# 64x64 products in all four corners of the PE array, and the decay of both recurrent states moved to ScalarE

## The reference

```python
def step(carry, inp):
    S, R = carry
    q_t, k_t, v_t, a_t, aR_t, b_t, g_t = inp
    kn = k_t / jnp.maximum(jnp.linalg.norm(k_t, axis=-1, keepdims=True), 1e-12)
    pred = jnp.einsum('bhji,bhj->bhi', S, kn)
    r = jnp.clip(v_t - pred, -CLIP, CLIP)
    S = a_t[..., None] * S
    kp = jnp.einsum('bhd,bhde->bhe', kn, S)
    S = S + b_t[..., None, None] * kn[..., None] * (v_t - kp)[..., None, :]
    o = jnp.einsum('bhji,bhj->bhi', S, q_t)
    R = aR_t[..., None] * R
    kpR = jnp.einsum('bhd,bhde->bhe', kn, R)
    R = R + g_t[..., None, None] * kn[..., None] * (r - kpR)[..., None, :]
    o = o + jnp.einsum('bhji,bhj->bhi', R, q_t)
    return ((S, R), o)
```

## Time and profile before

| | us |
|---|---|
| median of 3 runs | 3591.83 (3588.75 to 3591.98) |
| time of the profiled execution | 3588.82 |
| its span, first to last instruction | 3587.0 |
| of it the 32 chunks of the scan, about | 60 to 2690 |
| TensorE's mean granted clock, share of full speed | 0.911 |
| PE / DVE / ACT / POOL busy over the span | 88% / 76% / 48% / 34% |

### The profile page before, as it was taken

One profiled execution on the slowest core, in us unless ns is written; L12 is line 12 of the kernel. 1 busy time (PEld: TensorE's weight loads), 2 busy tenths in 40 slices (PEclk: granted clock), 3 DMA queues, 4 the chain that ended last, 5 costly groups with the idle time before them and its releaser, 6 DMA issues. The chain is left out here.

```text
span 3587.0 us, 134780 instructions
## 1 busy us (share of the span) xinstructions
PE 3170.7 (88%) x56922; PEld 2864.8 (80%) x56922; DVE 2724.0 (76%) x6995; ACT 1715.9 (48%) x4108; POOL 1212.5 (34%) x1001
## 2 busy tenths in 40 slices
PE   4999999999999999999999999999973998888880
PEld 4988888888888888888888898898862776667660
DVE  3888888899888888889888888888872444444445
ACT  2444554444444445544445444554421655555550
POOL 3112322222222223222222222322211666666664
PEclk8999899999999998999999999899985999999995
DMA  3211111111111111111111111111118777777766
GB/s 113 81 53 34 40 34 36 41 35 36 41 37 33 34 40 34 37 35 41 34 37 43 34 34 34 40 34 37 40 46 317 118 116 113 113 114 113 115 109 203
DMA packets 193472, 240.09 MB, mean 67 GB/s; under 512 B 26737, under 2 KB 171250, under 8 KB 192114
## 3 DMA queue, kind: packets, MB, share of 16 engines
q1 hardware_dynamic: 132896, 151.22, 13.7%
q0 software_dynamic: 58368, 75.80, 13.2%
q10 hardware_dynamic: 1618, 4.46, 0.3%
HBM read 96.17 MB, written 135.20 MB: 65 GB/s over the span
## 5 line engine op out<-in xcount | busy, mean ns | idle before, releaser
L383 POOL DMA_INDIRECT table<-xrow,place_i x256 | 264.1, 1032 | 800.1 <-DVE BR L846 191.7
L1080 POOL COPY inv_r<-N 32x512 f32<-32x512 f32 x128 | 136.5, 1067 | 798.7 <-DVE N L822 794.7
L1450 PE MATMUL bank<-w,route 128*128 x2560 | 371.3, 288 | 34.9 <-issue 10.8
L1450 PEld LDWEIGHTS bank<-w,route 128*128 128x128 f32 x2560 | 312.4, 192 | 104.2 <-issue 101.3
L449 DVE TENSOR_TENSOR tri<-tri,step 128x58 f32<-128x58 f32 (+13 forms) x896 | 305.4, 341 | 30.8
L448 DVE TENSOR_TENSOR step<-tri 128x58 f32<-128x58 f32 (+13 forms) x896 | 301.6, 337 | 26.4
L1465 PE MATMUL bank<-w,seen 128*128 x640 | 214.4, 417 | 51.2 <-DVE sh_sig L1538 9.7
L1526 DVE COPY to_row<-shared 128x1 int32<-128x1 int32 x228 | 35.1, 154 | 269.8 <-DMA acc<-sh_sig,to_row 39.5
L578 PE MATMUL bank<-xnT,wa 128*128 128x128 f32 x992 | 155.0, 330 | 67.5 <-ACT xnT L962 67.5
L578 PEld LDWEIGHTS bank<-xnT,wa 128*128 128x128 f32 x992 | 149.1, 242 | 71.6 <-ACT xnT L962 71.6
L637 PE MATMUL bank<-pq,c 64*64 64x128 f32 x2048 | 168.5, 339 | 0.0
(11 more groups left out here) (306 smaller groups left out, 9086.8 us busy)
## 6 DMA issues: line engine op xcount, KB each, us to landing
table<-blank SPq DMA_DIRECT2D x320, 129.0 KB
shared<-table SPq DMA_DIRECT2D x228, 129.0 KB
w<-in_wpack_dram SPq DMA_DIRECT2D x16, 1540.0 KB
xrow<-table SPq DMA_DIRECT2D x92, 129.0 KB
sum<-acc SPq DMA_DIRECT2D x16, 512.0 KB
acc<-blank SPq DMA_DIRECT2D x33, 128.0 KB, 3.1
x_rows<-y SPq DMA_DIRECT2D x64, 64.0 KB
x_res<-in_x_dram SPq DMA_DIRECT2D x64, 64.0 KB
```

Of the source, the lines that this page charges most:

```text
L383: nc.gpsimd.indirect_dma_start(out=table, out_offset=bass.IndirectOffsetOnAxis(ap=t.place8_i[:, k:k + 1], axis=0), in_=row[:, :], in_offse ...
L1080: ins = nc.gpsimd.tensor_copy(t.inv[1][r, :, Q * (q % 2):Q * (q % 2) + Q], t.N[r, 16:32, :])
L1450: mm = nc.tensor.matmul(ps[:, begin:begin + n], t.xT_slot[i % 3][:, P * kt:P * kt + P], weights(i, 257 * kt + begin, n), start=(kt == 0), ...
```

## The change

Products with 64x64 tiles are put in all four corners. `four` replaces `accumulate` and, for KS, KR, U, PR, W, A, O and RO, also `units`: it takes two banks at once and alternates between them. Every second unit (s = 1) is crossed: half j writes the partitions of the other half. for KS, KR, U, PR, W and A even units go to bank 0 and odd ones, crossed, to bank 1 (`crossed`). V, KRt, B ahead of U, BR, L and the inverses then hold their odd units with the halves exchanged, and the crossed groups U and W bring them back. For O and RO units 4a and 4a+1 go to bank 0 and 4a+2 and 4a+3, crossed, to bank 1. SU, RU, RQ, KT and PQ stay as they were. Copies and DVE operations that empty a bank address every second unit (`even_odd`) or every second pair of units (`by_pair`). V, the gates, `wo` and the bias are laid out to match. PR now waits for both U banks, RO for both W banks, and W for both halves of BR.

The two decays (DVE, lines 866 and 878) become `decay_state` on ACT: 16 activations of 128x64 each, with the decay of the unit as per-partition scale. The one of S stands behind the copies of O and ahead of the diagonal blocks, that of R behind the diagonal blocks and ahead of the copies of V.

```diff
--- before.py
+++ after.py
...
@@ -543,16 +552,33 @@
...
 
-            def accumulate(ps, h, pairs, first=False, last=False):
-
-                for i, u in enumerate(range(8 * h, 8 * h + 8)):
+            def four(banks, unit, pairs, first=True, last=True, whole=False):
+
+                for i in range(8):
                     for m, (lhsT, rhs) in enumerate(pairs):
-                        for j in range(2):
-                            r = slice(C * j, C * j + C)
-                            mm = nc.tensor.matmul(ps[r, C * i:C * i + C], lhsT(r, u), rhs(r, u),
-                                                  start=(first and i == 0 and m == 0),
-                                                  stop=(last and i == 7 and m == len(pairs) - 1))
-                return mm
+                        begin, end = m == 0, m == len(pairs) - 1
+                        if whole:
+                            begin, end = first and i == 0 and begin, last and i == 7 and end
+                        for s in range(2):
+                            u = unit(i, s)
+                            for j in range(2):
+                                r, to = slice(C * j, C * j + C), slice(C * (j ^ s), C * (j ^ s) + C)
+                                mm = nc.tensor.matmul(banks[s][to, C * i:C * i + C], lhsT(r, u), rhs(r, u),
+                                                      start=begin, stop=end)
+                            if s == 0:
+                                ins = mm
+                return ins, mm
+
+            def odd_unit(i, s):
+                return 2 * i + s
+
+            def pair_unit(i, s):
+                return 4 * (i // 2) + 2 * s + i % 2
+
+            def crossed(n, name, pairs):
+                banks = [begin(n, f"{name}0"), begin(n, f"{name}1")]
+                for ins in four(banks, odd_unit, pairs):
+                    ins.then_inc(t.sem["mm_done"], 1)
 
...
@@ -608,15 +634,13 @@
...
                 need(pe, t, "states_ready", 2 * n - 1)
-                for h in range(2):
-                    units(n, f"KS{h}", h, [(of(t.kplus[0]), of(t.S))])
+                crossed(n, "KS", [(of(t.kplus[0]), of(t.S))])
                 if front:
...
                 need(pe, t, "states_ready", 2 * n)
-                for h in range(2):
-                    units(n, f"KR{h}", h, [(of(t.kplus[1]), of(t.R))])
+                crossed(n, "KR", [(of(t.kplus[1]), of(t.R))])
                 if front:
...
@@ -678,12 +702,10 @@
...
                 pe.wait_ge(t.sem["inv_s_ready"], n + 1)
-                for h in range(2):
-                    units(n, f"U{h}", h, [(of(t.inv[0]), of(t.B))])
-                for h in range(2):
-                    wait_emptied(pe, t, o, n, f"U{h}")
-                    units(n, f"PR{h}", h, [(lambda r, u: t.pq[r, 0, u, :], of(t.S)),
-                                           (lambda r, u: t.pqT[r, u, 0, :], of(t.U))])
+                crossed(n, "U", [(of(t.inv[0]), of(t.B))])
+                wait_emptied(pe, t, o, n, "U1")
+                crossed(n, "PR", [(lambda r, u: t.pq[r, 0, u, :], of(t.S)),
+                                  (lambda r, u: t.pqT[r, u, 0, :], of(t.U))])
                 for h in range(2):
...
@@ -691,22 +713,20 @@
...
                         norm_matmul(nc, t, ps, i).then_inc(t.sem["front_mm"], 1)
-                for h in range(2):
-                    ins = accumulate(begin(n, f"O{h}"), h, [(of(t.S), lambda r, u: t.pq[r, 1, u, :]),
-                                                            (of(t.R), of(t.rqplus)),
-                                                            (of(t.U), lambda r, u: t.pqT[r, u, 1, :])], first=True)
-                ins.then_inc(t.sem["O_begun"], 1)
+                O = [begin(n, "O0"), begin(n, "O1")]
+                ins = four(O, pair_unit, [(of(t.S), lambda r, u: t.pq[r, 1, u, :]), (of(t.R), of(t.rqplus)),
+                                          (of(t.U), lambda r, u: t.pqT[r, u, 1, :])], last=False, whole=True)
+                ins[1].then_inc(t.sem["O_begun"], 1)
                 ps = begin(n, "SD")
...
                 pe.wait_ge(t.sem["inv_r_ready"], n + 1)
-                for h in range(2):
-                    pe.wait_ge(t.sem["BR_ready"], 2 * n + h + 1)
-                    units(n, f"W{h}", h, [(of(t.inv[1]), of(t.BR))])
-                for h in range(2):
-                    wait_emptied(pe, t, o, n, f"W{h}")
-                    accumulate(o.bank(t, n, f"O{h}"), h, [(of(t.B), of(t.rqT))], last=True).then_inc(t.sem["O_done"], 1)
+                pe.wait_ge(t.sem["BR_ready"], 2 * n + 2)
+                crossed(n, "W", [(of(t.inv[1]), of(t.BR))])
+                wait_emptied(pe, t, o, n, "W1")
+                for ins in four(O, pair_unit, [(of(t.B), of(t.rqT))], first=False, whole=True):
+                    ins.then_inc(t.sem["O_done"], 1)
                 for h in range(2):
...
@@ -789,7 +809,7 @@
...
                     ps = mm(n, f"KS{h}")
-                    nc.vector.tensor_tensor(t.B[:, half[h], :], t.V[:, half[h], :], blk(ps[:, :]),
+                    nc.vector.tensor_tensor(even_odd(t.B, h), even_odd(t.V, h), blk(ps[:, :]),
                                             ALU.subtract).then_inc(t.sem["dve_emptied"], 1)
...
@@ -835,15 +855,15 @@
...
                 for h in range(2):
-                    r, rest = t.BR[:, half[h], :], t.KRt[:, half[h], :]
+                    r, rest = even_odd(t.BR, h), even_odd(t.KRt, h)
                     ps = mm(n, f"PR{h}")
-                    nc.vector.tensor_tensor(r, t.V[:, half[h], :], blk(ps[:, :]),
+                    nc.vector.tensor_tensor(r, even_odd(t.V, h), blk(ps[:, :]),
                                             ALU.subtract).then_inc(t.sem["dve_emptied"], 1)
...
                     link(nc.vector.tensor_tensor(r, r, rest, ALU.subtract))
-                    nc.vector.tensor_tensor(r, r, bc(t.beta[n % 2][:, 1, half[h]], C), ALU.mult).then_inc(t.sem["BR_ready"], 1)
+                    nc.vector.tensor_tensor(r, r, bc(t.beta[n % 2][:, 1, h:16:2], C), ALU.mult).then_inc(t.sem["BR_ready"], 1)
                 if route:
...
@@ -862,9 +882,6 @@
...
                                             ALU.add).then_inc(t.sem["dve_emptied"], 1)
-                wait_emptied(dve, t, o, n, "SU1")
-                nc.vector.tensor_tensor(t.S[:], t.S[:], bc(t.dec_end[n % 2][:, 0, :], C),
-                                        ALU.mult).then_inc(t.sem["states_ready"], 1)
                 if front:
...
@@ -874,9 +891,6 @@
...
                                             ALU.add).then_inc(t.sem["dve_emptied"], 1)
-                wait_emptied(dve, t, o, n, "RU1")
-                nc.vector.tensor_tensor(t.R[:], t.R[:], bc(t.dec_end[n % 2][:, 1, :], C),
-                                        ALU.mult).then_inc(t.sem["states_ready"], 1)
                 if front:
...
@@ -948,6 +962,14 @@
...
 
+            def decay_state(n, g, state):
+                for h in range(2):
+                    wait_emptied(act, t, o, n, f"{'SR'[g]}U{h}")
+                    for u in range(8 * h, 8 * h + 8):
+                        ins = nc.scalar.activation(state[:, u, :], state[:, u, :], ACT.Copy,
+                                                   scale=t.dec_end[n % 2][:, g, u:u + 1])
+                ins.then_inc(t.sem["states_ready"], 1)
+
             empty_values(-1)
...
@@ -1038,13 +1060,16 @@
...
                 for h in range(2):
-                    empty(n, f"W{h}", t.B[:, half[h], :])
+                    empty(n, f"W{h}", even_odd(t.B, h))
                 for h in range(2):
                     act.wait_ge(t.sem["O_done"], 2 * n + h + 1)
-                    nc.scalar.copy(t.V[:, half[h], :], blk(o.bank(t, n, f"O{h}")[:, :])).then_inc(t.sem["out_emptied"], 1)
+                    nc.scalar.copy(by_pair(t.V[:], h), o.bank(t, n, f"O{h}")[:, :].rearrange("p (a b n) -> p a b n", b=2, n=C)).then_inc(t.sem["out_emptied"], 1)
+                decay_state(n, 0, t.S)
                 if front:
...
                     diagonal(n, 1)
+                decay_state(n, 1, t.R)
+                if front:
                     empty_values(n)
...
```

More of the change, by code:

```diff
@@ L302, in blk, with even_odd, by_pair @@
     return ap.rearrange("p (u n) -> p u n", n=C)
+def even_odd(x, h):
+    return x[:, h:16:2, :]
+def by_pair(x, h):
+    return x.rearrange("p (a s b) n -> p a s b n", s=2, b=2)[:, :, h, :, :]
 def route_scores(nc, t, link):
@@ L470, in gate_matmuls @@
         for j in range(2):
-            r = slice(C * j, C * j + C)
+            r = slice(C * (j ^ b), C * (j ^ b) + C)
             dst = ps[r, b:32 + b:2]
@@ L474, in gate_matmuls @@
                 nc.tensor.matmul(dst, t.xnT[:, kt, C * b:C * b + C], t.wbg[:, kt, j, :], start=(kt == 0), stop=False)
-            mm = nc.tensor.matmul(dst, t.ones_pair[C * j:C * j + 1, C * j:C * j + C],
-                                  t.bg_bias[C * j:C * j + 1, :, :].rearrange("p g u -> p (g u)")[:, b:32:2],
+            at = C * (j ^ b)
```

(19 more changed lines are left out.)

## The result

| | before | changed |
|---|---|---|
| median, us | 3591.9 (3588.75 to 3596.74, 4 runs) | 3480.49 (3479.21 to 3483.73, 4 runs) |
| profiled execution, its span, us | 3588.82, 3587.0 | 3481.59, 3479.8 |
| mean granted clock | 0.911 | 0.889 |

What follows compares the result with a forecast made beforehand. DVE's work was taken to set the pace, with PE through the chain after N. Terms -2.3 + 0.6 - 0.6 - 0.5 gave -2.8 us per chunk, -90 us in all, so 3500 us; 8-in-10 range 3440 to 3612.

Steps and rivals of the forecast that it cites:

- the likeliest case: Whole kernel: corners overlap, PE gets idle, DVE's work sets the pace; about 3500 us, own range 3440 to 3555, chance 0.53.
- (c): DVE's PQ waits: KR crossed brings PE sooner, but low-clock projections in every chunk delay banks; -0.6 us per chunk.
- (d): Chain after N: U halves, PR waits for both U copies, NS comes 1.1 us sooner; -0.5 us per chunk taken.
- A crossed group: PE products in four corners: 64 records take 1.0 us instead of 1.95, with V as the nearest row.
- (a) the decays: Both decays leave DVE: -2.3 us per chunk; on ACT 3.3 to 4.0 us per state, covered, priced at 0.
- (b): RU waits for SU0's bank; idle PE may run RU and A at the lower clock; +0.6 us per chunk.
- it should happen in all: Step of the PQ waits: about 3 us of PE idle time makes the `a` projections run low in all chunks.
- then takes 1.95: Step of the chain after N: PR starts at 1515.4 and takes 1.95 us instead of 3.8.
- The fourth case: Crossed groups: corners don't overlap, double waits stay; +0.4 us per chunk, 3605 us, slower, chance 0.2.
- The third case: RU, A, PR and SU run at low clock in each chunk; -0.2 us per chunk, about 3585 us, chance 0.13.
- PE's busy share: Profile after the change: PE, busy 88% of the span before, was to be busy near 80%.
- The norms' wait: DVE's wait for the key norms after N: was to fall from 2.8 to about 1 us per chunk.

Runs made afterwards that it cites:

- e1: The kernel before, with only the two decays moved to ScalarE and products straight as before: 3450.8 us, ratio 0.9626.
- e8: The changed kernel, with eight unused 128x128 identity products in PE's idle time ahead of RU: 3457.6 us, ratio 0.9664.
- e2: The changed kernel, with both decays put back on VectorE, so corners only: 3559.3 us, ratio 0.9926.
- e7: The kernel before, with nine unused 128x128 identity products in PE's idle time ahead of the `a` projections: 3534.4 us, ratio 0.9873.
- e3: The changed kernel, with PR in two passes, the one that needs no U ahead of the wait for the U copies: 3422.3 us, ratio 0.9559.
- e4: The changed kernel with every product straight, keeping paired banks, double waits and the decays on ScalarE: 3550.9 us, ratio 0.9915.
- e9: e6 plus eight unused 128x128 identity products ahead of the `a` projections: 3366.2 us, ratio 0.941.
- e6: The changed kernel with PR in two passes and NS moved ahead of SU: 3368.7 us, ratio 0.9411.

## Why the prediction was right

The time, its range, the sign and the likeliest case held. Its terms held less well than their sum, -2.8 us per chunk forecast and -3.33 measured: (c) gave 1.4 us more than forecast and (d) 0.8 less, and that these two errors have opposite signs is luck. Without (c)'s the chunk would have lost 2.0 us, some 60 us in all.

- **A crossed group**: 1.0 us forecast from V, 0.94 measured beside 1.86 straight, without the last record itself. V was the right row to go by. But the rate doesn't hold through all groups: over the 30 inner chunks the twelve crossed groups take 18.8 us together instead of 25.8, 7.0 us less where 11.4 were forecast. PR at the lower clock, and gaps in KS and O, took the rest; the share of these that counts is in (c) and (d). On the Trainium skill's rule in "TensorE: Matmul & The Clock Gate", Part 3, that weight loads overlap only with other row groups: this trace disagrees, since W's and RO's crossed tiles share rows and run at twice the rate. (The prediction points to this rival as the third case in two places; it is the fourth.)
- **(a) the decays**: right. -2.3 forecast, and the last link of e1 gave -2.48. 3.93 us for sixteen on ACT (forecast up to 4.0), and ACT sits idle 2.09 us after them.
- **(b) RU and A**: right in mechanism and size. (a) and (b) together were to give -1.7, and the last link gave -1.67; so (b) is +0.8 where +0.6 was forecast. RU runs at the lower clock at 3.39 us, in 28 of the 30 inner chunks, and e8, where it is 0 of 30 and the last link is e1's again (19.40 and 19.39), shows that the idle time in front is why.
- **(c) the PQ waits**: mis-sized, -0.6 forecast and -1.97 measured. The step that failed is "it should happen in all": PE was to idle about 3 us ahead of the `a` projections and run them at the lower clock in every chunk. It waits 0.49 us there in the chunk shown, and they take 3.84 us; they are low in 4 of the 30 inner chunks. I had moved DVE's part of the chunk by 2.3 us without asking what that does to PE's wait for it. The 1.4 us that RU loses to the clock in (b) also bring PE later, and so does KS, which was to take half and takes 2.5 us on average. The price was wrong too. e2 is the case that (c) described: the projections low in 27 of 30 chunks after 3.1 us of idle time. DVE waits 0.9 us per chunk for PQ there, not the 1.7 of the sum, because PQ itself then runs at full clock in 29 of 30. Before the change it was low in 26, and (c), which took the later banks as given, left that out. e1 and e7 show the mechanism from either side.
- **(d) the chain after N**: wrong in sign, -0.5 forecast and +0.31 measured. The wait for both U copies was priced about right: PR starts 10.2 us after the end of N on average, where 10.5 was forecast and 9.9 measured before. The step that failed is that PR "then takes 1.95" and SU 1.95, with 0.9 us for a low clock "in part of the chunks". PR runs at half clock in all 30 inner chunks and takes 3.60 us, SU is low in 17 and takes 2.63; so NS, forecast 1.1 us sooner, comes 0.3 us later, which is the link's +0.31. DVE's wait for PR is in every chunk (69.8 us, 32 times). The clamp of BR kept its rate (427 ns against 426). e3 filled the gap and took 1.88 us off.
- **The fourth case** (corners that don't overlap): e4 is that case, and it takes 3551 instead of 3605. Its sum left out the gain of (c), which needs no corners: 1.95 us per chunk in e1, 31 x 1.95 = 60 us, and 3605 - 60 = 3545. So it was not a case that ends slower than before, and its chance of 0.2 sat on the wrong side of no change. The price of the order was seen in the right places (PR behind U, A behind RU): 3.1 us per chunk against e1, 2.7 forecast.
- **The third case** (the clock takes the gain: RU, A, PR and SU low in each chunk) is in the result as well: RU and PR were low in nearly all chunks, SU in half of them, A in 7 of 30. It cost +0.8 and +0.31 us where that case had +1.6 and +0.5; what it left out is that (c) would pay it back.
- The mean clock fell below 0.911 and PE's busy share fell, as forecast, to 84% and not 80. The norms' wait is 1.6 us per chunk and not near 1.

That the decays give more than all of the gain (134 of 111 us) and that the corners cost 23 on top of them wasn't in the prediction; it had both halves as gains.

## What to carry to other kernels

Making an engine quicker pays only where another waits for it; with the decays off VectorE, the four corners first cost 23 us, since the order with its double waits took more than they gave, and were worth 126 once two moves had shortened the chain that the double waits sat on. When a change halves the length of groups, look at what the pairing makes wait, and put work that needs neither copy into the gap. And a shorter step on one engine can keep TensorE out of an idle gap and so at full clock: fill the gap with unused products once, as in e7, to see what it costs. Then count where the low stretches went, as e8 and e9 only moved them.

## What the runs showed of the hardware

Four 64x64 tiles in float32, which share rows in pairs and write the same PSUM partitions in pairs, in different banks, run at twice the rate of two (64 records in 1.16 against 2.08 us, of which the last record is 0.22). At half clock they run at about the rate of two at full clock (PR, 128 records in 3.5 against 3.8 us).

Crossed groups don't always keep that rate. KS of the changed kernel has gaps that the profile puts down to nothing:

```profile
1250.97 0.91 PE L566 MATMUL bank<-S,kplus 64*64 64x64 f32 x45
1252.24 0.35 PE L566 MATMUL bank<-S,kplus 64*64 64x64 f32 x5 [0.36 <-issue]
1252.98 0.51 PE L566 MATMUL bank<-S,kplus 64*64 64x64 f32 x14 [0.39 <-issue]
...
PEld bank L566 <- issue: 115.1, 240, 24.4
```

The group takes 2.5 us in this chunk, no less than a straight one, and 2.5 on average of the inner chunks. Weight loads of line 566 idle so for 115.1 us in 240 places over the span (24.4 of it once, at the start), and its products in 113 places; in e4, the same line with straight products, these are 62.2 us in 138 places (24.4 once) and 8:

```profile
PE bank L566 <- issue: 41.7, 113, 0.6
...
PE bank L566 <- issue: 1.9, 8, 0.4
```

For a part of the gaps the traces point at PE's own instructions. The page lists a DMA queue `q8 instruction` with 462 packets and 7.57 MB, 16 KB a packet; that is 66 bytes for each of PE's 113844 products and weight loads, and no other engine has nearly as many. In e6 a packet comes every 4.3 us of the scan. Between 80 and 2400 us e6 has 132 gaps of over 0.1 us in which PE neither multiplies nor loads weights and waits for nothing that the profile shows. They make 75 us, and 97 of them (58 us) end 1.2 to 1.7 us after such a packet has landed; by chance it would be about one in eight. This one comes right behind the dense products of O, and the packet landed at 1558.24:

```profile
1559.71 1.10 PE L428 MATMUL bank<-shared,sh_h 128*128 128x256 f32 x4 [1.04 <-issue]
```

That fits products issued faster than their instructions arrive, but no run tests it. It doesn't explain the gaps of KS above: only 1.2 of their 20.8 us end so. Their cause stays open.
